# Cross-attention and mixture of experts on one core: unit 0's query in two halves, a reordered start, two loads on ScalarE's queue, 23 more filler transposes

## The chip, the cores and the metric

One core of a Trainium2 chip. The metric is the device time of one execution in microseconds (us), lower is better. Five engines run programs of their own (TensorE, VectorE, ScalarE, GpSimd, SyncE) and meet at semaphores. The profile gives the clock that was granted to TensorE in every stretch as a share of its full 2.4 GHz; 0.50 is 1.2 GHz.

## What is computed

x is 4 batches of 1024 rows of 256 floats; each batch has a context of 77 rows of 256. All is in fp32.

```python
def attention(q, k, v, mask):                    # 16 heads of 16
    qh, kh, vh = heads(q @ w_q + b_q), heads(k @ w_k + b_k), heads(v @ w_v + b_v)
    scores = where(mask == 0, -10000.0, qh @ kh.T * 16 ** -0.5)
    return merge(softmax(scores) @ vh) @ w_o + b_o
x = x + tanh(g_x) * attention(layernorm(x), ctx, ctx, mask)
xf = layernorm(x)
comb = top 2 of 4 of softmax(xf @ gate_w.T), rescaled to a sum of 1
y = sum over e: comb[:, e] * ((silu(xf @ eg[e].T) * (xf @ eu[e].T)) @ ed[e].T)
y = y + (silu(xf @ sg.T) * (xf @ su.T)) @ sd.T   # 688 wide inside, as each expert
x = x + tanh(g_f) * y
```

## The kernel before

**Work and its order.** The 4096 rows are 16 units of 256 rows, two tiles of 128. A unit goes through the attention, its second layernorm and the shared expert; the routed experts follow in a part of their own ("big tiles"), which the change does not touch. Each engine's program is one list written out by hand: a start, then `first_steps()` for units 0 to 3, then steps for the later units. An engine takes its instructions strictly in the order of its list, and each waits on counts of semaphores. A DMA belongs to the queue of the engine that issues it (SPq is SyncE's, ACTq ScalarE's) and occupies that engine while it is issued.

**One unit n.** The step names are those of the code, with the engine of each:
- `load_x` (L997), `load_mask` (L1002), SyncE: 256 KB of x, 77 KB of mask. `stats_1` (VectorE, L2037 to L2042) makes mean and variance, `rstd1` (GpSimd, L1150 to L1155) the scale, then x is normalised into xh: by ScalarE for unit 0 (L1538), by GpSimd for the later units (L1282, L1285).
- `x_T` (TensorE, L2736): four transposes into the PSUM bank p_m; `xT_copy` (ScalarE, L1545) copies them out; `q_T` (TensorE, L2744): eight matmuls by W_q, again into p_m.
- The query is kept as two parts of fewer bits each: `q_hi` (ScalarE, L1551) rounds p_m plus b_q, `q_lo` (VectorE, L2090) is the rest. p_m is free for its next user when q_lo has run; `prob_v(n)` waits for `q_lo(n + 2)`, for it uses p_m too.
- `scores(n, j)` (TensorE, L2763), j from 0 to 3: quarter j is tile j % 2 against the eight heads of half m = j // 2, which need only half m of the query and of the keys. It takes six matmuls (hi by hi, hi by lo, lo by hi, for two groups of four heads) into banks of p_s. `half_max(n, j)` (VectorE, L2108 and L2112) puts the masked entries to -10000 and takes the maxima; `exps(n, j)` (ScalarE, L1564) makes eight exps with their sums; `recip` (VectorE) and `normalise` (GpSimd, L1174) divide.
- `prob_T` (TensorE, L2782) and `t_copy` (ScalarE) transpose the probabilities; `prob_v(n)` (TensorE, L2797): 32 small matmuls against vblk. `out_proj`, `attended` and the second layernorm follow.

**The start.** SyncE loads, in this order, x of unit 0 (L997), the context (308 KB, L1054), W_k (256 KB, L1055), mask 0 (77 KB), W_q (256 KB, L1057), W_v (256 KB, L1058), x of unit 1, the gate's weights, mask 1, the shared expert's gate and up matrices (L1065, L1067), W_o, x of units 2 to 5, mask 2. ScalarE issues b_k and b_q (1 KB each, L1638, L1639), b_v (spread over 77 partitions, 77 KB, L1640), the two gates tgx and tgf (0.5 KB each) and b_o (128 KB, L1643). b_k, b_q and b_v count on one semaphore, s_bias, and both the keys (`keys_T`, L2185) and the query wait for all three (48 counts).

Keys: TensorE transposes the context (L2967 for batch 0, L2972 for the others; VectorE copies it out at L2196, L2199) and `keys_of` multiplies by W_k (L2979), batch 0 first. `keys_T` adds b_k and scales; ScalarE rounds (L1647, later L1655 for batches 1 to 3), VectorE takes the rest (L2191). The keys of a batch are then spread into blocks, one per half of the heads: `key_hi(m)` (VectorE, L2172) and `key_block` (GpSimd, L1178). Values: `values_of_context(half)` (TensorE), `context_values(k)` (VectorE, L2213, into vall); when both are done (s_vall 2), `place_values` (SyncE, L1013) copies batch 0's into vblk with 24 small DMAs within SBUF. `rest_of_start` (VectorE) is keys_T for batches 1 to 3, gwT, and two products with the gates.

`keep_warm(n)` (TensorE, L2962) is n transposes of the identity into p_t, whose result nobody reads; the kernel has 20 while x is loaded, two before keys_of and four before q_T(0). `w_T`, `w_hi` and `w_lo` transpose the shared expert's weights and split them in two parts; 11 groups of them lie between the steps of the first units.

The lists before, for unit 0 (each continues with unit 1):

```python
# VectorE: keys_T(0, 1); no_sight(0); keys_lo; key_hi(0); key_hi(1); q_lo(0); stats_1(1); then
half_max(0, 0) rest_of_start() context_values(0) context_values(1) half_max(0, 1) no_sight(1) stats_1(2)
half_max(0, 2) recip(0, 0) q_lo(1) recip(0, 1) w_lo(0) half_max(0, 3) w_lo(1) recip(0, 2) w_lo(2)
# ScalarE: normed(0); xT_copy(0); first keys rounded; q_hi(0); two tanh; then
exps(0, 0) xT_copy(1) other_keys_hi() exps(0, 1) q_hi(1) w_hi(0) exps(0, 2) w_hi(1) w_hi(2) exps(0, 3)
# TensorE: context transposes; keys_of(0, 1); x_T(0); q_T(0); keys_of(1, 4); gate's transposes; then
scores(0, 0) values_of_context(0), (1) scores(0, 1) x_T(1) scores(0, 2) q_T(1) w_T(0) scores(0, 3) w_T(1) w_T(2)
```

## Time and profile before

| | before |
|---|---|
| runs, us | 869.85, 868.10, 867.94; median 868.10 |
| profiled execution, us | 869.38 |
| its span, us | 867.7 |
| mean granted clock of TensorE | 0.991 |
| TensorE matmuls busy | 837.4 us, 97% |
| TensorE weight loads | 733.5 us, 85% |
| VectorE | 585.3 us, 67% |
| ScalarE | 522.0 us, 60% |
| GpSimd | 468.8 us, 54% |

The metric is the execution's time; the span goes from the first to the last instruction of the profile, and 1.7 us lie around it. Times in the trace count from the span's start. The shares are means over the whole span: they tell which engine is full most of the time and not what holds up a given step. A matmul's end is modelled, so a busy TensorE need not be at its peak.

### The profile page before, as it was taken

How to read it: one execution, taken by the hardware profiler on the slowest of the kernel's cores; microseconds unless marked ns; L12 is line 12 of the kernel's file. 1: busy time of each engine (PE TensorE's matmuls, PEld its weight loads, DVE VectorE, ACT ScalarE, POOL GpSimd, SP SyncE). 2: the span in 40 equal slices, each digit the busy share in tenths (PEclk: the TensorE clock that was granted, in tenths of full speed). 3: DMA queues.
4: the chain of work that ended last, by engine and by line, in shares of the span. 5: the costliest groups of instructions: out<-in, count | busy, mean ns of one | idle time of the engine just before them, and what ended most of it. 6: DMA issues, size and time to landing. Idle time of an engine off the chain costs nothing.

```text
span 867.7 us, 19215 instructions
## 1 busy us (share of the span) xinstructions
PE 837.4 (97%) x6183; PEld 733.5 (85%) x6184; DVE 585.3 (67%) x1214; ACT 522.0 (60%) x1846; POOL 468.8 (54%) x562
## 2 busy tenths in 40 slices
PE   8788899999999999999999999999999999999994
PEld 6567788888888799999988888888888888889994
DVE  6889889898888657976565666655665655454442
ACT  3989999999999635646565544445445454323231
POOL 5678678697575443666631444444444424364442
PEclk9899999999999999999999999999999999999998
DMA  7124323232222232323351444443444432232221
GB/s 222 41 79 122 117 68 98 85 106 83 76 90 63 75 109 71 119 91 113 102 153 39 76 75 71 69 65 64 69 68 68 73 50 38 31 49 42 36 42 19
DMA packets 104761, 67.84 MB, mean 78 GB/s; under 512 B 63514, under 2 KB 93055, under 8 KB 104671
## 3 DMA queue, kind: packets, MB, share of 16 engines
q1 hardware_dynamic: 90743, 48.93, 20.0%
q0 software_dynamic: 12864, 17.57, 12.6%
q8 instruction: 48, 0.79, 0.4%
q14 instruction: 42, 0.34, 0.1%
q10 hardware_dynamic: 1064, 0.21, 0.1%
HBM read 34.78 MB, written 25.82 MB: 70 GB/s over the span
## 4 chain that ended last, share of the span: by engine, by line
PE 86%; ACT 5%; DVE 3%; issue 2%; DMA 2%; POOL 0%; SPq 0%; DVEq 0%; ACTq 0%; POOLq 0%
PE p_s L680 23%; PE p_f L697 12%; PE p_f L2852 9%; PE p_s L347 7%; PE p_f L2897 4%; PE p_s L2852 4%; PE p_t L2782 3%; PE p_s L2763 3%; ACT prob L1564 3%; PE p_t L358 3%; PE p_m L2797 3%; PE p_m L2744 3%; PE p_m L2809 3%; PE p_s L2897 2%; PE p_s L2955 1%
## 5 line engine op out<-in xcount | busy, mean ns | idle before, releaser
L1564 ACT ACTIVATE prob<-p_s,negmax 128x77 f32<-128x77 f32 x512 | 161.7, 376 | 7.8 <-DVE negmax L2112 7.7
L1564 ACT ACTIVATION_READ_ACCUMULATOR prob<-p_s,negmax 128x1 f32 x512 | 129.9, 258 | 0.0
L537 POOL DMA_INDIRECT big_xin<-xn_scratch,slot_id x52 | 52.2, 1004 | 125.2 <-DMA big_placed<-big_xin 87.8
L581 ACT ACTIVATE big_sil<-p_s 128x512 f32<-128x512 f32 (+1 forms) x78 | 46.5, 596 | 115.7 <-PE p_s L680 102.2
L680 PE MATMUL p_s<-big_fxT_hi,big_w_hi 128*128 128x512 f32 (+1 forms) x286 | 112.8, 395 | 0.1
L680 PE MATMUL p_s<-big_fxT_lo,big_w_hi 128*128 128x512 f32 (+1 forms) x286 | 112.9, 395 | 0.0
L680 PE MATMUL p_s<-big_fxT_hi,big_w_lo 128*128 128x512 f32 (+1 forms) x286 | 112.2, 392 | 0.0
L1174 POOL TENSOR_TENSOR prob<-prob,rinv 128x616 f32<-128x616 f32 x64 | 78.9, 1237 | 58.6 <-DVE rinv L2119 58.6
L545 POOL DMA_INDIRECT out_rows<-big_yout,slot_id x52 | 85.9, 1652 | 43.8 <-DVE big_yout L643 28.2
L626 DVE TENSOR_TENSOR big_hid<-p_s,big_sil 128x512 f32<-128x512 f32 (+1 forms) x78 | 54.0, 692 | 76.8 <-ACT big_sil L581 72.0
L697 PE MATMUL p_f<-wd_hi,big_hT_hi 128*128 (+1 forms) x312 | 85.5, 280 | 0.0
L697 PE MATMUL p_f<-wd_lo,big_hT_hi 128*128 (+1 forms) x312 | 85.3, 279 | 0.0
L1193 POOL TENSOR_TENSOR shT_lo<-shid,shT_hi 128x256 fp32r<-128x256 f32 x80 | 63.2, 803 | 38.1 <-ACT shT_hi L1606 37.8
L2852 PE MATMUL p_f<-xnT_hi,swgu_hi 128*128 128x256 f32 x240 | 73.0, 304 | 0.0
L697 PE MATMUL p_f<-wd_hi,big_hT_lo 128*128 x260 | 72.7, 280 | 0.0
L633 DVE TENSOR_TENSOR big_hT_lo<-big_hid,big_hT_hi 128x512 fp32r<-128x512 f32 (+1 forms) x65 | 44.9, 691 | 35.6 <-ACT big_hT_hi L586 32.1
L2852 PE MATMUL p_f<-xnT_hi,swgu_lo 128*128 128x256 f32 x240 | 67.4, 281 | 0.0
L2852 PE MATMUL p_f<-xnT_lo,swgu_hi 128*128 128x256 f32 x240 | 67.3, 280 | 0.0
L680 PEld LDWEIGHTS p_s<-big_fxT_hi,big_w_lo 128*128 128x128 f32 (+1 forms) x286 | 53.0, 185 | 13.0
L586 ACT ACTIVATE big_hT_hi<-big_hid 128x512 fp32r<-128x512 f32 (+1 forms) x78 | 49.3, 632 | 23.2 <-DVE big_hid L626 18.8
L680 PEld LDWEIGHTS p_s<-big_fxT_hi,big_w_hi 128*128 128x128 f32 (+1 forms) x286 | 53.1, 186 | 10.3 <-issue 0.3
L2108 DVE COPY_PREDICATED_SCALAR p_s<-blind,hidden 128x616 f32 x64 | 54.8, 856 | 10.2 <-PE p_s L2763 9.7
(348 smaller groups left out, 2539.7 us busy)
## 6 DMA issues: line engine op xcount, KB each, us to landing
big_placed<-big_xin SPq DMA_DIRECT2D x176, 32.0 KB
xr<-in_x SPq DMA_DIRECT2D x16, 256.0 KB, 2.8
x_scratch<-xr SPq DMA_DIRECT2D x16, 256.0 KB, 2.4
xn_scratch<-xn SPq DMA_DIRECT2D x16, 256.0 KB, 2.1
xt_scratch<-xnT SPq DMA_DIRECT2D x16, 256.0 KB, 3.2
xin<-xt_scratch SPq DMA_DIRECT2D x16, 256.0 KB, 3.4
x1in<-x_scratch SPq DMA_DIRECT2D x16, 256.0 KB, 3.3
out_rows<-syout SPq DMA_DIRECT2D x16, 256.0 KB, 2.2
```

The lines of the kernel that those rows point to most:

```text
L347: last = nc.tensor.matmul(p_gu[:, g0:g1], fxT[a][:, c, :], wgu[b][:, bass.ds(e * KC + c, 1), g0:g1], start=(c == 0 and q == 0), stop=(c == ...
L537: pool.indirect_dma_start(xin[:, t, :], None, v["xn_d"], bass.IndirectOffsetOnAxis(slot_id[:, column(j, t)], 0)).then_inc(s_rows, 16)
L545: pool.indirect_dma_start(out, bass.IndirectOffsetOnAxis(slot_id[:, column(j, t)], 0), yout[:, t, :], None, compute_op=ALU.add).then_inc(s ...
L626: nc.vector.tensor_tensor(hid[n % 2][0:r, :], up, sil[n % 2][0:r, :], ALU.mult).then_inc(s_hid, 1)
L680: last = nc.tensor.matmul(p_gu[c % 2][half][0:out_rows, :], lhsT, fxT[j % 2][x][:, :, k, :], start=(k == 0 and q == 0), stop=(k == KC - 1 ...
L697: last = nc.tensor.matmul(p_y[t // 2][:, t % 2 * H:(t % 2 + 1) * H], hT[n % 3][h][0:r, at], wd[w][0:r, bass.ds(e * FC + c, 1), :], start=( ...
L1174: pool.tensor_tensor(pr_, pr_, rinv[:, t, m * HH:(m + 1) * HH].unsqueeze(2).broadcast_to([P, HH, SK]), ALU.mult).then_inc(s_P, 1)
L1193: pool.tensor_tensor(hT[1][:, c, :], hid[:, c, :], hT[0][:, c, :], ALU.subtract).then_inc(s_hlo, 1)
L1564: last = act.activation(prob[n % 2][t][:, m * PW + h * SK:m * PW + (h + 1) * SK], p_s[:, 2 * t + h // 4, col:col + SK], ACT.Exp, bias=negm ...
L2108: nc.vector.copy_predicated(sc, blind[:, n % 2, t, :].unsqueeze(1).unsqueeze(1).broadcast_to(shape), hidden[:, :].unsqueeze(2).unsqueeze(3 ...
L2852: last = nc.tensor.matmul(bank[:, j * UT * P:(j + 1) * UT * P], swgu[w][:, k, j * SGU + c * P:j * SGU + (c + 1) * P], xns[x][:, n % 2, k, ...
L2897: nc.tensor.matmul(bank[:, t * H:(t + 1) * H], hT[x][:, c, at], swd[w][:, c, :], start=(c == 0 and q == 0), stop=False)
```

## The change

**Loads.** The context and W_q are issued from ScalarE, ahead of b_k, b_q and b_v. SyncE's list is x, W_k, mask, W_v, x of unit 1 and so on.

**The query of unit 0** is made by halves. q_T(0) puts half 0 into p_m as before and half 1 into the bank p_f[1], and signals after each; q_hi(0) and q_lo(0) do and signal each half. For the later units nothing is split; only the counts grow by one (`queries(n)` is n + 2). scores(0, 0) and scores(0, 1) need half 0 alone, and key block 0 alone; scores(0, 2) needs both.

**The order of the lists.** VectorE makes key_hi(0) and half 0 of q_lo(0), then takes half_max(0, 0) and half_max(0, 1), and only then key_hi(1), the other half of q_lo, rest_of_start, half_max(0, 2), both context_values, recip(0, 0), no_sight(1), stats_1(2) and half_max(0, 3). ScalarE has exps(0, 1) ahead of xT_copy(1), and each later quarter one place earlier. TensorE has scores(0, 0) and scores(0, 1) right after q_T(0), ahead of keys_of(1, 4) and the gate's transposes; values_of_context(1), whose bank is p_f[1], waits for both halves of q_lo.

**Filler transposes.** 4 before scores(0, 3), 4 between w_T(0) and w_T(1), 9 between w_T(1) and w_T(2), 6 before scores(1, 0): 23. They use p_t, so TensorE waits before the first of them for the keys of all batches and for gwT, which are read from there.

```diff
         def four_banks(n, c):
             return n >= LATE or (n == LATE - 1 and c >= 2)
 
+        def queries(n):
+
+            return n + 2
+
+        def q_bank(n, m):
+            return p_f[1][:, 0:UT * P] if n == 0 and m == 1 else p_m[:, m * UT * P:(m + 1) * UT * P]
+
         def f_bank(n, c):
             use = 7 * n + c + (c >= 2)
             return wide_f[use % 4] if four_banks(n, c) else p_f[use % 2]
...
                 load_matrix(sp, v, raw[q % 2], s_raw[q % 2], q)
 
             load_x(0)
-            sp.dma_start(ctx_sb[:, :, :], v["ctx_in"].rearrange("b k d -> k b d")).then_inc(s_ctx, 16)
             sp.dma_start(wk[:, :, :], v["w_k"].rearrange("(c p) d -> p c d", p=P)).then_inc(s_wk, 16)
             load_mask(0)
-            sp.dma_start(wq[:, :, :], v["w_q"].rearrange("(c p) d -> p c d", p=P)).then_inc(s_wq, 16)
             sp.dma_start(wv[:, :, :], v["w_v"].rearrange("(c p) d -> p c d", p=P)).then_inc(s_wv, 16)
             load_x(1)
             sp.dma_start(gw_sb[:, :], v["gate_w"]).then_inc(s_gw, 16)
...
 
             def xT_copy(n):
                 act.wait_ge(s_xT, n + 1)
-                wait(act, s_q, n)
+                wait(act, s_q, queries(n - 1) if n > 0 else 0)
                 act.activation(xT[:, :, :], cols(p_m[:, :]), ACT.Copy).then_inc(s_xTc, 1)
 
             def q_hi(n):
-                act.wait_ge(s_q, n + 1)
                 wait(act, s_S, 4 * (n - 1))
                 for m in range(KC):
-                    last = act.activation(qT[0][:, n % 2, m, :], p_m[:, m * UT * P:(m + 1) * UT * P], ACT.Identity,
-                                          bias=bq[:, m:m + 1])
+                    if n == 0 or m == 0:
+                        act.wait_ge(s_q, m + 1 if n == 0 else queries(n))
+                    last = act.activation(qT[0][:, n % 2, m, :], q_bank(n, m), ACT.Identity, bias=bq[:, m:m + 1])
+                    if n == 0 and m == 0:
+                        last.then_inc(s_qhi, 1)
                 last.then_inc(s_qhi, 1)
 
             def exps(n, j, h0=0, h1=HH):
...
                 dst, src = e_part(G, 0)
                 act.activation(dst, src, ACT.Copy).then_inc(s_ehi, 1)
 
+            act.dma_start(ctx_sb[:, :, :], v["ctx_in"].rearrange("b k d -> k b d")).then_inc(s_ctx, 16)
+            act.dma_start(wq[:, :, :], v["w_q"].rearrange("(c p) d -> p c d", p=P)).then_inc(s_wq, 16)
             act.dma_start(bk[:, :], v["b_k"].rearrange("(c p) -> p c", p=P), allow_slow_non_contiguous=True).then_inc(s_bias, 16)
             act.dma_start(bq[:, :], v["b_q"].rearrange("(c p) -> p c", p=P), allow_slow_non_contiguous=True).then_inc(s_bias, 16)
             act.dma_start(bv[:, :], v["b_v"].partition_broadcast(SK)).then_inc(s_bias, 16)
...
 
             def first_steps():
                 exps(0, 0)
+                exps(0, 1)
                 xT_copy(1)
                 other_keys_hi()
-                exps(0, 1)
+                exps(0, 2)
                 q_hi(1)
                 w_hi(0)
-                exps(0, 2)
+                exps(0, 3)
                 w_hi(1)
                 w_hi(2)
-                exps(0, 3)
 
                 t_copy(0, 0)
                 w_hi(3)
...
+            def q_half_lo(n, m):
+                return nc.vector.scalar_tensor_tensor(
+                    out=qT[1][:, n % 2, m, :], in0=q_bank(n, m), scalar=bq[:, m:m + 1], in1=qT[0][:, n % 2, m, :],
+                    op0=ALU.add, op1=ALU.subtract)
+
             def q_lo(n):
-                dve.wait_ge(s_qhi, n + 1)
-                for m in range(KC):
-                    last = nc.vector.scalar_tensor_tensor(
-                        out=qT[1][:, n % 2, m, :], in0=p_m[:, m * UT * P:(m + 1) * UT * P], scalar=bq[:, m:m + 1],
-                        in1=qT[0][:, n % 2, m, :], op0=ALU.add, op1=ALU.subtract)
-                last.then_inc(s_qlo, 1)
+                dve.wait_ge(s_qhi, queries(n))
+                q_half_lo(n, 0)
+                q_half_lo(n, 1).then_inc(s_qlo, 1)
 
             def no_sight(n):
                 dve.wait_ge(s_mask[n % 2], 16 * (n // 2 + 1))
...
             no_sight(0)
             keys_lo(0, 1, 0)
             dve.wait_ge(s_own, 3)
-            for m in range(KC):
-                key_hi(m)
-            q_lo(0)
+            key_hi(0)
+            dve.wait_ge(s_qhi, 1)
+            q_half_lo(0, 0).then_inc(s_qlo, 1)
             stats_1(1)
 
             def context_values(k):
...
 
             def first_steps():
                 half_max(0, 0)
+                half_max(0, 1)
+                key_hi(1)
+                dve.wait_ge(s_qhi, queries(0))
+                q_half_lo(0, 1).then_inc(s_qlo, 1)
                 rest_of_start()
+                half_max(0, 2)
                 context_values(0)
                 context_values(1)
-                half_max(0, 1)
+                recip(0, 0)
                 no_sight(1)
                 stats_1(2)
-                half_max(0, 2)
-                recip(0, 0)
+                half_max(0, 3)
                 q_lo(1)
                 recip(0, 1)
                 w_lo(0)
-                half_max(0, 3)
                 w_lo(1)
                 recip(0, 2)
                 w_lo(2)
...
             def x_T(n):
                 pe.wait_ge(s_xh, n + 1)
                 wait(pe, s_x1, n - 2)
-                wait(pe, s_qlo, n)
+                wait(pe, s_qlo, queries(n - 1) if n > 0 else 0)
                 for k in range(KC):
                     for t in range(UT):
                         last = nc.tensor.transpose(p_m[:, (k * UT + t) * P:(k * UT + t + 1) * P],
...
                 pe.wait_ge(s_xTc, n + 1)
                 for m in range(KC):
                     for k in range(KC):
-                        last = nc.tensor.matmul(p_m[:, m * UT * P:(m + 1) * UT * P], wq[:, k, m * P:(m + 1) * P],
+                        last = nc.tensor.matmul(q_bank(n, m), wq[:, k, m * P:(m + 1) * P],
                                                 xT[:, k, :], start=(k == 0), stop=(k == KC - 1))
+                    if n == 0 and m == 0:
+                        last.then_inc(s_q, 1)
                 last.then_inc(s_q, 1)
 
             def scores(n, j):
                 t, m = j % 2, j // 2
                 b = n // UB
                 wait(pe, s_exp, 4 * n + j - 1)
-                if j == 0:
-                    pe.wait_ge(s_qlo, n + 1)
+                if n == 0 and j == 0:
+                    pe.wait_ge(s_qlo, 1)
+                elif j == 0 or (n == 0 and j == 2):
+                    pe.wait_ge(s_qlo, queries(n))
                 if b == 0:
                     pe.wait_ge(s_kbhi, m + 1)
                     pe.wait_ge(s_kblo, m + 1)
...
-                pe.wait_ge(s_qlo, min(n + 3, NU))
+                pe.wait_ge(s_qlo, queries(min(n + 2, NU - 1)))
...
             x_T(0)
             keep_warm(4)
             pe.wait_ge(s_wq, 16)
+            pe.wait_ge(s_ctxT, 1 + KC)
             q_T(0)
-            pe.wait_ge(s_ctxT, 1 + KC)
+            scores(0, 0)
+            scores(0, 1)
             keys_of(1, B, p_t)
             pe.wait_ge(s_gw, 16)
             for k in range(KC):
...
                 last.then_inc(s_vps, 1)
 
             def first_steps():
-                scores(0, 0)
                 values_of_context(0)
-                values_of_context(1)
-                scores(0, 1)
                 x_T(1)
                 scores(0, 2)
+                pe.wait_ge(s_qlo, queries(0))
+                values_of_context(1)
                 q_T(1)
+                pe.wait_ge(s_kT, 4)
+                pe.wait_ge(s_gwT, 2)
+                keep_warm(4)
+                scores(0, 3)
                 w_T(0)
-                scores(0, 3)
+                keep_warm(4)
                 w_T(1)
+                keep_warm(9)
                 w_T(2)
+                keep_warm(6)
 
                 scores(1, 0)
                 w_T(3)
```

## Rows read from the trace of the kernel before

**Rows 1.** Stretches of 20 us: engines' busy us (instructions), PEclk, DMA share, GB/s.

```profile
60.00:80.00 20.00, 17.78 (x184) 12.96 (x173) 18.55 (x37) 19.14 (x102) 15.31 (x21) 1.00 0.34 107
...
100.00:120.00 20.00, 19.98 (x184) 17.03 (x183) 17.86 (x41) 18.86 (x93) 16.50 (x25) 1.00 0.29 85
```

**Rows 2.** Timeline of the DMA issues: start, duration in us, queue, line.

```profile
0.81 0.50 ACTq L1638 DMA_DIRECT2D bk<-in_L_xattn_b_k  x1
...
1.32 0.45 SPq L1054 DMA_DIRECT2D ctx_sb<-in_ctx  x1
...
2.76 0.47 SPq L1057 DMA_DIRECT2D wq<-in_L_xattn_w_q  x1
...
3.27 0.59 SPq L1058 DMA_DIRECT2D wv<-in_L_xattn_w_v  x1
...
3.45 0.64 ACTq L1643 DMA_DIRECT2D bog<-in_L_xattn_b_o  x1
```

**Rows 3.** Timeline, 9 to 14 us: start, us, engine, line; in brackets idle before.

```profile
8.96 0.50 DVE L2185 TENSOR_SCALAR kT<-p_s,bk 128x77 f32<-128x77 f32 x2 [0.95 <-PE p_s L2979]
9.12 0.47 PEld L2962 LDWEIGHTS p_t<-ident 128*128 128x128 f32 x4
...
9.43 0.60 ACT L1545 ACTIVATE xT<-p_m 128x512 f32<-128x512 f32 x1 [0.75 <-PE p_m L2736]
9.92 0.33 ACT L1647 ACTIVATE kT_hi<-kT 128x154 fp32r<-128x154 f32 x1
...
10.52 2.53 DVE L2172 TENSOR_TENSOR kblk_hi<-kT_hi,own 128x616 fp32r<-128x616 f32 x2
10.75 3.38 POOL L1178 TENSOR_TENSOR kblk_lo<-kT_lo,own 128x616 fp32r<-128x616 f32 x2 [3.19 <-DVE kT_lo L2191]
...
10.98 1.99 PE L2744 MATMUL p_m<-xT,wq 128*128 128x256 f32 x8 [1.16 <-DMA wq<-in_L_xattn_w_q]
...
13.08 0.84 ACT L1551 ACTIVATE qT_hi<-p_m,bq 128x256 fp32r<-128x256 f32 x2 [2.83 <-PE p_m L2744]
```

**Rows 4.** Timeline, 15 to 22 us: first maximum, first and second exps, the context's values.

```profile
15.86 0.86 DVE L2108 COPY_PREDICATED_SCALAR p_s<-blind,hidden 128x616 f32 x1
...
17.59 0.33 ACT L1564 ACTIVATE prob<-p_s,negmax 128x77 f32<-128x77 f32 x1 [3.49 <-DVE negmax L2112]
...
18.72 1.29 DVE L2213 TENSOR_TENSOR vall<-p_f,bv 77x512 f32<-77x512 f32 x2
...
21.73 0.33 ACT L1564 ACTIVATE prob<-p_s,negmax 128x77 f32<-128x77 f32 x1 [0.23 <-DVE negmax L2112]
```

**Rows 5.** Timeline of SyncE's queue, 18 to 62 us.

```profile
20.04 18.75 SPq L1013 DMA_DIRECT2D vblk<-vall  x24
```

**Rows 6.** Timeline of TensorE: prob_v(0), prob_v(1).

```profile
42.12 3.61 PE L2797 MATMUL p_m<-pT,vblk 128*32 128x256 f32 x32 [0.46 <-DVE qT_lo L2090]
...
59.96 1.93 PE L2797 MATMUL p_m<-pT,vblk 128*32 128x256 f32 x32
```

**Rows 7.** Short stretches, columns as in rows 1.

```profile
24.00:28.00 4.00, 1.80 (x12) 1.13 (x12) 3.57 (x8) 4.00 (x23) 3.77 (x6) 1.00 0.07 7
...
34.00:35.00 1.00, 1.00 (x5) 0.82 (x4) 0.44 (x2) 1.00 (x7) 0.82 (x1) 0.50 0.05 5
38.00:42.00 4.00, 2.25 (x16) 1.52 (x16) 3.62 (x7) 4.00 (x26) 2.06 (x2) 1.00 0.45 103
...
43.00:45.00 2.00, 2.00 (x25) 1.22 (x20) 1.14 (x5) 2.00 (x14) 1.24 (x2) 0.50 0.11 17
```

**Rows 8.** DMA issues in 0 to 22 us: median us from issue to landing.

```profile
wv<-in_L_xattn_w_v SPq DMA_DIRECT2D x1, 256.0 KB, 8.6
```

**Rows 9.** Chain of waits: start, us, what; one quarter of scores.

```profile
77.50 0.69 PE p_s L2763 x6
```

**Rows 10.** Timeline of GpSimd, 24 to 38 us.

```profile
25.57 1.04 POOL L1285 TENSOR_TENSOR xh<-xh,nb 128x512 f32<-128x512 f32 x1
```

**Rows 11.** Line 1013 alone, 18 to 62 us: duration ns min/median/max.

```profile
L1013 SPq DMA_DIRECT2D vblk<-vall x30: 545/756/954, 20.0 to 43.9; - x30
```

More of the change, by code:

```diff
@@ L2816, in xn_T @@
                 pe.wait_ge(s_x1, n + 1)
-                pe.wait_ge(s_qlo, min(n + 4, NU))
+                pe.wait_ge(s_qlo, queries(min(n + 3, NU - 1)))
                 for k in range(KC):
```

## The prediction

> **What bounds it now.** The page's first part has TensorE busy for nearly all of the span, so the next question is where it is not. Stretches of 20 us answer: 17.8 of 20 us from 60 to 80, and 19.98 from 100 to 120 [rows 1]; of the 34 such stretches from 120 to 800 only one is under 19.3. From about 100 us on TensorE has no gap, so the change can only move the time at which that full stretch begins, one for one; the steps behind it are unaltered. Before 100 us ScalarE is the fullest (19.1 of 20 us, [rows 1]), fed by VectorE's maxima. The start is what the diff rewrites, so I read it as a timeline, and set the changed order's durations end to end against it.
>
> The start has four marks. W_q's load is issued at 2.76 and TensorE waits for it until 10.98 [rows 2, 3]. The first exps begin at 17.59, the context's values are done at 20.0, and at 20.04 SyncE starts 24 DMA issues that put them into vblk; they take 18.75 us [rows 4, 5]. prob_v(0), the first reader of vblk, runs at 42.12 after q_lo(2), for 3.61 [rows 6]. The clock is at its lower level (1.2 GHz, granted 0.50) at 34 to 35 and again at 43 to 45, and at the upper one in the 4 us before each of the two falls, in which TensorE was busy for 1.80 and 2.25 us [rows 7].
>
> **Loads.** Before, SyncE issues x, context, W_k, mask, W_q; context (0.45) and W_q (0.47) go to the head of ScalarE's queue, ahead of b_k, b_q, b_v, which so leave 1.0 later [rows 2]. ScalarE has time: its issues ended at 4.1 [rows 2], and the copy of x's transposes had waited 0.75 when it ran at 9.43 [rows 3]. SyncE's later loads leave 0.5 to 1.0 earlier. W_q passes the mask and no longer decides: the end of that copy does, at 10.03, plus some 0.2 for sharing with the context. What gets late is b_v. keys_T(0, 1) needs the three biases; it ran at 8.96, so they had landed by then [rows 3]. Now 564 KB stand before them in their own queue. Until W_q landed at 10.94, 1153 KB of SyncE's loads (x 256, context 308, W_k 256, mask 77, W_q 256, by the tensors' sizes) and 208 KB of ScalarE's had gone with it: 134 KB per us from the first issues at 0.81. If the two queues take turns, 643 KB of each must pass before b_v is in: 1286 KB, or 10.4 us. Bounds: 9.0 (no delay) and 11.9 (when W_v, behind as much, landed: 3.27 plus 8.6, [rows 2, 8]). I take 10.5. The Trainium skill, page "DMA: Bandwidth & Descriptors", section "Issuing engines are not separate DMA queues", says that DMAs of all engines share the same 16 engines, and that a second issuer saves issue time alone; by it the context and W_q are paid for by what stands behind them, and the sum would have b_v at the late bound, 1.4 us more. The rows do show the two queues in flight together, and no more.
>
> **Unit 0.** Keys 0.50, their rounded copy 0.33, the rest as much, one key block on GpSimd 1.7 at most [rows 3]: 10.5 + 2.9 = 13.4. Half of the query is there by 12.3, since q_T is 2.0 whole and q_hi 0.43 a half. scores(0, 0) 13.4 to 14.1 (0.69, [rows 9]); maximum 1.7 (15.86 to the exp's start, [rows 4]); exps(0, 0) at 16.0 where it was 17.59: 1.6 earlier. The second maximum ends at 17.7 and its exps(0, 1), now at 21.73 [rows 4], follow exps(0, 0) without the gap, at 18.2: 3.5 earlier. So far the change does what it says.
>
> **What is queued behind it on VectorE.** After the second maximum (17.7) come key_hi(1) 1.0 (2.53 for two beside GpSimd's, [rows 3]), half of q_lo 0.45, rest_of_start 1.1 (17.6 to 18.72), half_max(0, 2) 1.7 and its wait 0.2, and only then both context_values 1.3 [rows 4]: they end at 23.4, which was 20.0. stats_1(2) stands behind them and ends at 24.8; GpSimd's xh(2), made from it, is then ready at 28.8 instead of 26.6, and normalise(0, 0) starts that much later [rows 10]. The lead is gone by unit 1.
>
> **SyncE.** Its 24 issues move with the values: 23.4 + 18.75 = 42.2, and the last piece lands about 1.1 later (between 0 and the 3.3 between the last issue's end and prob_v(0), which did not wait for it). prob_v(0) so starts at 43.3 and not at 42.12: 1.2 later. Here one wait takes the place of another, and all slack of the way to it is swallowed, the cold clock's too.
>
> **Fillers.** 23 transposes at 0.117 (0.47 for four, [rows 3]) are 2.7 us of TensorE. Four stand before scores(0, 3), whose reader VectorE is free at 24.9 while the scores are done at 24.85; 13 stand between w_T(0) and w_T(2), which wait for ScalarE's exps and VectorE's rounding; six before scores(1, 0), 2 us ahead of its maximum. I cost them at nothing; if that cover were gone, at 0.47, 1.5 and 0.7. They fill the stretch before the first fall of the clock [rows 7] and should keep it at 2.4 GHz up to 35. What that gives on TensorE ends in the wait for vblk. Nothing is put into 36 to 43, where TensorE has the same 2.25 of 4 us as now, or less with the wait at its end. So I expect the second fall again, with prob_v(0) at 3.6 us and not the 1.93 of prob_v(1) at the upper level [rows 6].
>
> **Sum.** prob_v(0) starts 1.2 later; being later, its end reaches back into the upper level, minus 0.3; the rest follows one for one: 0.9 later. The profiled execution took 869.4 (span 867.7 and 1.7 around it), so a like execution gives 870.3. The median of the three runs is 868.1, 1.3 below that; nothing ties the 1.3 to the start, so I carry it: 869.0. As a run without the first fall loses nothing of what varies there, I put 869.2. Two thousandths (1.7 us, 866.4 and 869.8) is about what a measurement of this kernel can tell from no change.
>
> **Rivals.** (a) *The clock holds through prob_v(0).* For it: fillers before, and only 1.2 us more of gap. Against: the 2.25 of 4 us. 43.3 + 1.93 = 45.2 against 45.7: 0.5 earlier, 867.7. (b) *Slower: the biases.* If b_v lands at 12.0, ScalarE's copy, both key blocks, all maxima and the values go 1.5 later, prob_v(0) starts at 44.8, and the longer gap keeps the lower level over scores(2, 0) and out_proj(0) too (some 1.9 us of matmuls at the upper): 2.7 later at its start, 2.0 to 3.5 at its end: 871.0. It decides once the biases are later than 10.5. (The skill's section "Queues, rings and completion order" on the same page has each DMA engine take turns between queues packet by packet; the tiny packets of b_k and b_q would then each cost a turn against 1 KB of SyncE's.) (c) *Faster: vblk is not late.* The issues took 545 to 954 ns each [rows 11]. At 545, 24 of them end at 36.5 and prob_v(0) waits for q_lo(2) only, at 41.9; with the clock up it ends at 43.8, 1.9 earlier: 866.2. It decides below 0.72 us an issue, and needs the clock as well. (d) *The change does not do what it says*: the biases are so late that exps(0, 0) stays at 17.6; that is the end of (b).
>
> **Chances.** The forecast 0.42 (0.08 of it above 869.8), (a) 0.15, (b) 0.28, (c) 0.15. Faster is (c) 0.15; slower is (b) and the top of the forecast, 0.36; the rest, 0.49, is the same. The range goes from 866.9 (part of (c) left out) to 871.6 (the early half of (b)'s late end in). The forecast's own is 868.2 to 870.4.
>
> **What would show it.** keys_T(0, 1) waiting for a DMA until about 10.5, scores(0, 0) near 13.4, exps(0, 0) near 16.0; values done at 23.4 and SyncE's vblk issues from there to 42.2; prob_v(0) near 43.3 with its waiting put down to a DMA; the clock whole at 28 to 35 and at 0.50 again at 43 to 45; TensorE full from about 101. It is wrong if keys_T is not delayed, if prob_v(0) starts before 42.5, or if prob_v(0) takes 1.9.

## The result, and the profile after

| | before | after |
|---|---|---|
| runs on the same chips, median us | 868.62 (13 runs) | 871.32 (13 runs) |
| profiled execution, us | 869.38 | 871.42 |
| its span, us | 867.7 | 869.7 |
| TensorE matmuls busy, us | 837.4 | 839.7 |
| VectorE busy, us | 585.3 | 585.2 |

The ratio is 1.0030, with a 95% interval of 1.0022 to 1.0038: the change makes the kernel 2.7 us slower. No engine's busy time grew by more than the fillers. The time is lost before 48 us and carried to the end: scores(2, 0) starts 1.66 later (47.31 against 45.65) and scores(5, 2) 1.69 later (106.57 against 104.88), one for one as the prediction had it. The two profiled executions differ by 2.0 and not by 2.7: before's lay 0.8 above its median, after's 0.1.

The start, from the timeline of the changed kernel (columns as in [rows 3]):

```profile
9.71 0.50 DVE L2196 TENSOR_SCALAR kT<-p_s,bk 128x77 f32<-128x77 f32 x2 [2.19 <-DMA bv<-in_L_xattn_b_v]
...
10.55 0.60 ACT L1550 ACTIVATE xT<-p_m 128x512 f32<-128x512 f32 x1 [1.21 <-PE p_m L2750]
...
11.29 1.64 PE L2758 MATMUL p_m<-xT,wq 128*128 128x256 f32 x4
...
13.54 0.48 DVE L2097 SCALAR_TENSOR_TENSOR qT_lo<-p_m,bq,qT_hi 128x256 fp32r<-128x256 f32 x1 [1.11 <-ACT qT_hi L1557]
...
16.79 0.33 ACT L1571 ACTIVATE prob<-p_s,negmax 128x77 f32<-128x77 f32 x1 [2.30 <-DVE negmax L2123]
```

Against [rows 3] and [rows 4]: the keys waited 2.19 us for b_v and ran at 9.71 instead of 8.96, the copy of x's transposes at 10.55 instead of 9.43. The first exp still comes 0.80 earlier, at 16.79, since only half of the query is needed; the second quarter's exps followed at 19.21 instead of 21.73.

What came of that lead stands on VectorE and GpSimd, 21 to 35 us of the timeline:

```profile
21.40 0.86 DVE L2119 COPY_PREDICATED_SCALAR p_s<-blind,hidden 128x616 f32 x1 [0.43 <-PE p_s L2781]
...
23.01 1.27 DVE L2224 TENSOR_TENSOR vall<-p_f,bv 77x512 f32<-77x512 f32 x2
...
26.52 0.86 DVE L2119 COPY_PREDICATED_SCALAR p_s<-blind,hidden 128x616 f32 x1 [0.95 <-PE p_s L2781]
...
28.24 1.04 POOL L1290 TENSOR_TENSOR xh<-xh,nb 128x512 f32<-128x512 f32 x1
...
29.24 3.57 POOL L1179 TENSOR_TENSOR prob<-prob,rinv 128x616 f32<-128x616 f32 x3
...
31.05 0.34 DVE L2174 TENSOR_TENSOR swgu_lo<-p_f,swgu_hi 128x176 fp32r<-128x176 f32 x1 [1.39 <-ACT swgu_hi L1624]
...
32.15 1.15 DVE L2202 TENSOR_TENSOR kT_lo<-kT,kT_hi 128x462 fp32r<-128x462 f32 x1
33.22 0.85 DVE L2119 COPY_PREDICATED_SCALAR p_s<-blind,hidden 128x616 f32 x1
```

The last row is half_max(1, 0): 33.22, where it was 30.55. VectorE is to be seen waiting three times (0.43, 0.95, 1.39) where it had been nearly full. The same stretch of both kernels, from the start of half_max(0, 0) to the start of half_max(1, 0), says it in two rows (columns as in rows 1). Before:

```profile
15.86:30.55 14.69, 11.90 (x70) 8.38 (x69) 13.93 (x30) 12.46 (x70) 13.53 (x22) 0.93 0.25 75
```

After:

```profile
15.06:33.22 18.16, 15.87 (x103) 12.03 (x103) 15.06 (x32) 13.64 (x73) 13.52 (x22) 1.00 0.24 73
```

The stretch is 3.47 us longer. VectorE is busy 1.13 more in it (15.06 against 13.93: key_hi(1), 1.17, and half of q_lo, 0.47, now lie inside instead of ahead; other steps take less, keys_lo by 0.18) and idle 2.34 more (3.10 against 0.76).

Two ways lead to half_max(1, 0). One goes over GpSimd: stats_1(2) stands behind half_max(0, 2) and both context_values in VectorE's new list, xh(2) is made from it, and normalise(0, 0) can start only then, 12.45 behind the first exp instead of 8.98. That is the same 3.47. The other goes over ScalarE, which now has w_hi(1) and w_hi(2) behind exps(0, 3) (first its timeline in the changed kernel, then that of the kernel before):

```profile
28.25 0.33 ACT L1571 ACTIVATE prob<-p_s,negmax 128x77 f32<-128x77 f32 x1 [1.12 <-DVE negmax L2123]
...
30.67 0.84 ACT L1624 ACTIVATE swgu_hi<-p_f 128x176 fp32r<-128x176 f32 x2
```

```profile
27.74 0.92 ACT L1617 ACTIVATE swgu_hi<-p_f 128x176 fp32r<-128x176 f32 x2
```

w_hi(1), the first of the two in that row, starts 13.88 behind the first exp instead of 10.15, and w_lo(1) on VectorE waits 1.39 for it.

The rest of the way, from the timeline of TensorE, VectorE and SyncE:

```profile
24.32 18.75 SPq L1020 DMA_DIRECT2D vblk<-vall  x24
...
38.14 0.63 PE L2800 MATMUL p_t<-ident,prob 128*128 128x128 f32 x4 [1.65 <-ACT pT L1580]
...
39.84 1.09 PE L2800 MATMUL p_t<-ident,prob 128*128 128x128 f32 x4 [0.46 <-ACT pT L1580]
...
41.71 1.09 PE L2800 MATMUL p_t<-ident,prob 128*128 128x128 f32 x4 [0.78 <-ACT pT L1580]
...
43.44 0.87 DVE L2097 SCALAR_TENSOR_TENSOR qT_lo<-p_m,bq,qT_hi 128x256 fp32r<-128x256 f32 x2
...
44.45 2.93 PE L2815 MATMUL p_m<-pT,vblk 128*32 128x256 f32 x32 [0.27 <-DVE qT_lo L2097]
```

And short stretches (columns as in rows 1):

```profile
9.00:12.00 3.00, 2.60 (x10) 2.22 (x11) 1.25 (x5) 1.16 (x3) 0.13 (x1) 0.50 0.73 234
...
28.00:32.00 4.00, 2.64 (x22) 1.91 (x20) 2.57 (x8) 3.26 (x18) 3.92 (x5) 1.00 0.05 4
...
36.00:38.00 2.00, 0.48 (x3) 0.08 (x1) 1.41 (x4) 2.00 (x12) 1.48 (x2) 1.00 0.06 5
38.00:42.00 4.00, 2.63 (x16) 1.90 (x17) 2.96 (x7) 3.96 (x17) 2.92 (x6) 0.71 0.04 4
42.00:46.00 4.00, 3.73 (x28) 2.38 (x30) 3.05 (x5) 3.51 (x24) 0.72 (x1) 0.50 0.39 84
```

The fillers kept the clock up at 28 to 35, where it had fallen. In this execution it was also at the lower level at 9 to 12, where it had been up before. It now falls at 39.7 and stays at the lower level to 46.5 (28.6 to 35.4 and 42.2 to 45.6 before): the two groups of transposes behind the fall take 1.09 instead of 0.63. prob_v(0) runs at 44.45 and waits for q_lo(2); vblk's last piece had landed at 44.18, only 0.27 ahead.

**The sum by marks.** Single executions differ by 1 to 2 us in how early the loads land and where the low clock lies at the start, so I measure from the first exp, exps(0, 0). Starts behind it, in us:

| | exps(0, 0) at | exps(0, 3) | half_max(1, 0) | exps(1, 0) | prob_v(0) | scores(2, 0) |
|---|---|---|---|---|---|---|
| before | 17.59 | 10.82 | 12.96 | 14.68 | 24.52 | 28.06 |
| after | 16.79 | 11.45 | 16.43 | 18.15 | 27.66 | 30.52 |

So 0.80 is won up to the first exp, 3.47 is lost from there to exps(1, 0), and 1.01 is won between exps(1, 0) and scores(2, 0) (12.37 against 13.38): 1.66 in all. Of the 1.01, 0.68 is prob_v(0) itself, 2.93 us instead of 3.61, since the clock is back at its upper level from 46.5 on, before it ends; 0.33 lies ahead of it.

### The profile page after: what moved, and what is told of

Same layout as the page of the kernel before. It is cut to its first block, busy times and chain, and to the rows that moved or that the text cites. A ratio compares the mean times of both kernels' runs of the same rounds, so it can differ in the third digit from the quotient of the medians.

```text
span 869.7 us, 19263 instructions
## 1 busy us (share of the span) xinstructions
PE 839.7 (97%) x6206; PEld 735.2 (85%) x6207; DVE 585.2 (67%) x1214; ACT 522.3 (60%) x1846; POOL 467.1 (54%) x562
## 3 DMA queue, kind: packets, MB, share of 16 engines
q0 software_dynamic: 12864, 17.57, 12.5%
## 4 chain that ended last, share of the span: by engine, by line
PE 86%; ACT 4%; DVE 4%; issue 2%; DMA 1%; POOL 1%; DVEq 0%; SPq 0%; ACTq 0%; POOLq 0%
PE p_s L680 23%; PE p_f L697 12%; PE p_f L2870 9%; PE p_s L347 7%; PE p_f L2915 4%; PE p_s L2870 4%; PE p_t L2800 3%; PE p_s L2781 3%; PE p_t L358 3%; PE p_m L2827 3%; PE p_m L2815 3%; ACT prob L1571 3%; PE p_m L2758 2%; PE p_s L2915 2%; PE p_s L2973 1%
## 5 line engine op out<-in xcount | busy, mean ns | idle before, releaser
L1571 ACT ACTIVATION_READ_ACCUMULATOR prob<-p_s,negmax 128x1 f32 x512 | 132.3, 264 | 0.0
L581 ACT ACTIVATE big_sil<-p_s 128x512 f32<-128x512 f32 (+1 forms) x78 | 46.5, 596 | 114.9 <-PE p_s L680 114.9
L545 POOL DMA_INDIRECT out_rows<-big_yout,slot_id x52 | 85.2, 1638 | 43.3 <-DVE big_yout L643 29.6
L697 PE MATMUL p_f<-wd_hi,big_hT_lo 128*128 x260 | 72.7, 280 | 0.0
```

The costliest lines, as they stand in the source:

```text
L545: pool.indirect_dma_start(out, bass.IndirectOffsetOnAxis(slot_id[:, column(j, t)], 0), yout[:, t, :], None, compute_op=ALU.add).then_inc(s ...
L697: last = nc.tensor.matmul(p_y[t // 2][:, t % 2 * H:(t % 2 + 1) * H], hT[n % 3][h][0:r, at], wd[w][0:r, bass.ds(e * FC + c, 1), :], start=( ...
L1571: last = act.activation(prob[n % 2][t][:, m * PW + h * SK:m * PW + (h + 1) * SK], p_s[:, 2 * t + h // 4, col:col + SK], ACT.Exp, bias=negm ...
```

## The experiments

The theories to tell apart: prob_v(0) is late because of vblk (the forecast's), because of the clock, because of the loads, or because of the chain over VectorE and GpSimd that ends in exps(1, 0) and q_lo(2). Ratios are to the kernel before, run beside each group of experiments: 868.51 us for e1 to e4, 868.23 for e5 to e8, 868.29 for e9 to e12. Each kernel has one profile, so the marks rest on one execution each.

**e1: no fillers.** The changed kernel, its four keep_warm calls in first_steps left out.

```diff
-                keep_warm(4)
                 scores(0, 3)
                 w_T(0)
-                keep_warm(4)
                 w_T(1)
-                keep_warm(9)
                 w_T(2)
-                keep_warm(6)
```

> The changed kernel without its 23 filler transposes. Theory (a chain on VectorE and ScalarE sets prob_v(0)): four fillers stand between q_T(1) and scores(0, 3), whose maximum VectorE waited 0.95 us for, so exps(0, 3) and all behind it move up by up to 0.5; without fillers the clock is at its lower level somewhere in 28 to 35 again, as in the kernel before. Both effects are small and of opposite sign: 870.8 to 871.6 us. Rival (the clock decides): the fillers saved the fall at 28 to 35 but the fall at 39.7 to 46.5 took its place; without them the fall sits at 28 to 35, prob_v(0) takes about 2 us at the upper level: 870.0 or less.

Measured 870.82 us, 1.0026 (1.0016 to 1.0036) of the kernel before. exps(0, 3) comes 11.03 behind the first exp instead of 11.45, so four fillers did cost 0.42. half_max(1, 0) and exps(1, 0) did not move: 16.42 and 18.14. Something else than the chain over exps(0, 3) held them. The rows, from this kernel's timeline of GpSimd and VectorE:

```profile
28.07 3.56 POOL L1179 TENSOR_TENSOR prob<-prob,rinv 128x616 f32<-128x616 f32 x3
...
30.55 1.57 DVE L2202 TENSOR_TENSOR kT_lo<-kT,kT_hi 128x462 fp32r<-128x462 f32 x1
```

keys_lo started 0.43 earlier against the first exp and took 1.57 instead of 1.15. It ended at 32.12, 0.49 behind GpSimd's third normalise (31.63). After: 33.30 and 32.81, again 0.49.

The clock was at its lower level at 28.5 to 35.3 and 42.1 to 45.5, as in the kernel before, and scores(2, 0) still came 12.38 behind exps(1, 0), against 12.37 with the fillers: the 1.01 won there doesn't come from the first fall's absence.

**e2: loads back**, and **e3: loads only.** The change's two lines, undone in the changed kernel and made alone in the kernel before.

```diff
             load_x(0)
+            sp.dma_start(ctx_sb[:, :, :], v["ctx_in"].rearrange("b k d -> k b d")).then_inc(s_ctx, 16)
             sp.dma_start(wk[:, :, :], v["w_k"].rearrange("(c p) d -> p c d", p=P)).then_inc(s_wk, 16)
             load_mask(0)
+            sp.dma_start(wq[:, :, :], v["w_q"].rearrange("(c p) d -> p c d", p=P)).then_inc(s_wq, 16)
...
-            act.dma_start(ctx_sb[:, :, :], v["ctx_in"].rearrange("b k d -> k b d")).then_inc(s_ctx, 16)
-            act.dma_start(wq[:, :, :], v["w_q"].rearrange("(c p) d -> p c d", p=P)).then_inc(s_wq, 16)
```

> The changed kernel with context and W_q loaded from SyncE again. Theory: the moved loads made x (first statistics 5.55 instead of 4.89), the biases (keys_T at 9.71 instead of 8.96) and the copy of x's transposes (10.55 instead of 9.43) late and lowered the clock at 9.0 to 12.4; with them back q_T(0) runs at 10.98 at the upper level, scores(0, 0) at 13.1, exps(0, 0) at 15.8, and the whole chain to prob_v(0), the values and their 24 issues among it, comes 1.0 earlier: 870.4 us. Rival (the lead is lost behind unit 0 anyway, at half_max(1, 0), by waits that don't go back to the start): exps(0, 0) earlier by 1.0 but prob_v(0) by under 0.3: 871.2.

> The kernel before with only the two loads moved to ScalarE. Theory: keys and the transposes of x 1.1 later, key blocks done at 14.5, q_lo(0) at 15.1, scores(0, 0) at 15.3 instead of 14.88, and 0.4 to 1.1 later for everything up to prob_v(0): 869.1 to 869.7 us. Rival (the loads are harmless, W_q's earlier landing makes up for it): 868.6.

e2 took 871.20 us (1.0028, 1.0017 to 1.0040), e3 869.28 (1.0008, 0.9997 to 1.0019). Neither differs clearly from the kernel it was made of. e2's profile shows why a single one can't decide: its clock was at the lower level up to 14.05, so its first exp came at 17.52, later than after's. From exps(0, 0) to exps(1, 0) it took 18.16, e3 14.68: the loads have no part in the 3.47.

**e4: fillers only.** The kernel before with the 23 fillers (and their wait for p_t) among w_T(0), w_T(1), w_T(2) and scores(1, 0).

```diff
                 q_T(1)
+                pe.wait_ge(s_kT, 4)
+                pe.wait_ge(s_gwT, 2)
+                keep_warm(4)
                 w_T(0)
                 scores(0, 3)
+                keep_warm(4)
                 w_T(1)
+                keep_warm(9)
                 w_T(2)
+                keep_warm(6)
```

> The kernel before with only the 23 fillers, at the same places among the weights' transposes. If the clock is what the fillers buy: no lower level in 28 to 35, the transposes and scores(1, 1) there at full speed, and prob_v(0) no earlier than q_lo(2), which waits for ScalarE's exps, so 0 to 0.6 earlier there. Theory: as in the changed kernel the fall moves behind them, to 38 to 46, and gives it back: 868.3 to 869.0 us. Rival: the clock stays up through prob_v(0) as well, which then ends 1.9 earlier: 866.7.

867.85 us, 0.9990 (0.9980 to 1.0000): somewhat better than expected, at the edge of what can be told. The clock stayed up from 11.0 to 41.75 and fell there; prob_v(0) took 3.60 once more. scores(2, 0) came 27.14 behind the first exp, 0.92 less than before.

**e5: vblk early.** The changed kernel; SyncE's issues for batch 0 wait for the first half of the values, and VectorE makes that half earlier.

```diff
-                sp.wait_ge(s_vall, 2)
+                sp.wait_ge(s_vall, 2 if b > 0 else 1)
...
                 q_half_lo(0, 1).then_inc(s_qlo, 1)
+                context_values(0)
                 rest_of_start()
                 half_max(0, 2)
-                context_values(0)
                 context_values(1)
```

> The changed kernel with vblk's 24 issues set free by the first half of the values alone, whose sum VectorE makes right behind the query's second half. The issues run from about 20.7 to 39.5 and the last piece lands near 40.6 instead of 44.18. My theory now: prob_v(0) waits for q_lo(2), which is late because GpSimd's third normalise ends 16.0 after the first exp (12.5 before) and holds VectorE's keys_lo and half_max(1, 0) behind it; so nothing is gained: exps(1, 0) 18.1 to 18.4 behind exps(0, 0), 871.0 to 871.6 us. Rival (the forecast's own: vblk is the wait that sets prob_v(0)): prob_v(0) 1.2 earlier, 870.1.

**e6: keys_lo late.** The changed kernel with one line moved on VectorE.

```diff
-                keys_lo(1, B, 1)
 
                 half_max(1, 0)
+                keys_lo(1, B, 1)
```

> The changed kernel with keys_lo of batches 1 to 3 behind half_max(1, 0) on VectorE instead of ahead of it. Theory: keys_lo took 1.15 because it waited for GpSimd's normalise to end (it ended 0.48 or 0.49 behind it in three kernels); behind half_max(1, 0), with GpSimd idle, it takes under 0.8, and half_max(1, 0) starts 15.4 behind exps(0, 0) instead of 16.43: exps(1, 0) 1.0 earlier. prob_v(0) then waits for vblk, 0.25 earlier: 871.0 us. Rival (ScalarE's exps(0, 3) and w_hi set the pace): half_max(1, 0) no earlier than 16.2.

**e7: both.**

```diff
-                sp.wait_ge(s_vall, 2)
+                sp.wait_ge(s_vall, 2 if b > 0 else 1)
...
+                context_values(0)
                 rest_of_start()
...
                 half_max(1, 0)
+                keys_lo(1, B, 1)
```

> Both edits together. Theory of two waits side by side at prob_v(0) (q_lo(2) at 44.3, vblk at 44.2): only both together give the time back, prob_v(0) 0.9 to 1.0 earlier against exps(0, 0) than in the changed kernel: 870.4 us. Rival (the clock's fall at 39.7 eats it, since TensorE's gaps stay): under 0.3, 871.1.

e5: 870.78 us (1.0030, 1.0021 to 1.0039). vblk had landed at 40.23, 4 us ahead, and prob_v(0) started where it did, 27.68 behind the first exp:

```profile
44.36 2.97 PE L2815 MATMUL p_m<-pT,vblk 128*32 128x256 f32 x32 [0.27 <-DVE qT_lo L2097]
```

e6: 871.36 us (1.0041, 1.0027 to 1.0056). half_max(1, 0) moved to 15.39 and exps(1, 0) to 17.14, 1.01 earlier, and prob_v(0) only to 27.50. Now it waits for the DMA, from VectorE's and TensorE's timeline of e6:

```profile
29.95 0.34 DVE L2174 TENSOR_TENSOR swgu_lo<-p_f,swgu_hi 128x176 fp32r<-128x176 f32 x1 [1.39 <-ACT swgu_hi L1624]
...
31.05 0.85 DVE L2119 COPY_PREDICATED_SCALAR p_s<-blind,hidden 128x616 f32 x1
...
32.65 0.63 DVE L2202 TENSOR_TENSOR kT_lo<-kT,kT_hi 128x462 fp32r<-128x462 f32 x1
...
43.15 3.39 PE L2815 MATMUL p_m<-pT,vblk 128*32 128x256 f32 x32 [1.25 <-DMA vblk<-vall]
```

So GpSimd's way gave back 1.0 of the 3.47. half_max(1, 0) (31.05) now starts right behind w_lo(2), and w_lo(1) still waits 1.39 for w_hi(1). The other 2.4 stands with the way over ScalarE. No run put w_hi(1) and w_hi(2) back ahead of exps(0, 3), so that part is read from the rows and not shown. In the changed kernel w_T(1) had ended at 27.23, and ScalarE stood idle for the 1.12 before exps(0, 3).

e7: 870.01 us (1.0022, 1.0013 to 1.0031). prob_v(0) at 26.57 and scores(2, 0) at 29.45, 1.07 earlier than after. Each wait alone gives nothing (0.02 the wrong way and 0.16), both together 1.09: they stand side by side, and the forecast named only one. The 1.09 rests on the marks of one profile each. The whole times agree with it but don't prove it, since e7's interval still overlaps the change's (1.0022 to 1.0038). keys_lo itself takes 0.63 with GpSimd idle: 0.52 of its 1.15 was waiting for normalise, which no row puts down as a wait. The Trainium skill has a rule for it on the page "SBUF — State Buffer", section "Who interferes with whom": a tensor_tensor of VectorE with both inputs in SBUF contends with GpSimd's reads of SBUF, the port pair that the two share is an exclusive lock, and the order of issue decides which of them blocks. The traces agree: in all eleven profiles in which keys_lo runs beside normalise it takes 1.14 to 1.57 and ends 0.49 or 0.50 behind it, and in the other three it takes 0.63.

**e8: late fillers.** The kernel before with e4's 23 fillers and 14 more ahead of prob_T(0, 3), prob_T(0, 4) and prob_v(0), where TensorE waited; they write into banks whose last reader is waited for.

```diff
+            def warm_f(k, done, count):
+                pe.wait_ge(s_wlo, done)
+                for n in range(count):
+                    nc.tensor.transpose(p_f[k][:, n % 4 * P:(n % 4 + 1) * P], ident[:, :], ident[:, :])
...
                 scores(1, 2)
+                warm_f(1, 4, 3)
                 prob_T(0, 3)
+                warm_f(1, 4, 8)
                 prob_T(0, 4)
                 w_T(5)
                 scores(1, 3)
+                warm_f(0, 5, 3)
                 prob_v(0)
```

> The kernel before with the 23 fillers and 14 more in the gaps ahead of prob_T(0, 3), prob_T(0, 4) and prob_v(0), in banks that nobody holds there. Theory: TensorE is busy through 36 to 42, the clock does not fall there, prob_v(0) takes 1.93 instead of 3.6, and scores(2, 0) comes 1.5 to 2.0 earlier: 866.0 to 866.9 us. Rival (the fillers delay what stands behind them as much as the clock gives): 867.9, as with the 23 alone.

865.73 us, 0.9969 (0.9959 to 0.9978): 2.5 us faster than the kernel before and, by the two ratios, some 5.3 faster than the change. Its windows and prob_v(0):

```profile
38.00:42.00 4.00, 3.57 (x40) 2.40 (x42) 3.62 (x7) 4.00 (x27) 1.79 (x2) 1.00 0.54 127
42.00:46.00 4.00, 3.47 (x38) 2.37 (x31) 3.46 (x10) 4.00 (x26) 3.39 (x4) 1.00 0.34 97
```

```profile
40.89 1.93 PE L2797 MATMUL p_m<-pT,vblk 128*32 128x256 f32 x32
```

TensorE is busy for 3.57 of the 4 us in which it had been busy for 2.25 [rows 7], the clock is at its upper level without a break from 5.5 to 858.8 us, and prob_v(0) takes 1.93. scores(2, 0) is at 25.46, 2.60 earlier than before and 1.68 earlier than e4.

**e9 and e10: late fillers on the changed kernel**, alone and with e7's two edits. As in e8, with 12 more ahead of prob_T(0, 2), since TensorE waits 1.65 there.

```diff
                 q_T(2)
+                warm_f(1, 4, 12)
                 prob_T(0, 2)
                 scores(1, 2)
+                warm_f(1, 4, 3)
                 prob_T(0, 3)
+                warm_f(1, 4, 8)
                 prob_T(0, 4)
                 w_T(5)
                 scores(1, 3)
+                warm_f(0, 5, 3)
                 prob_v(0)
```

> The changed kernel with 26 more fillers in TensorE's gaps ahead of prob_T(0, 2), prob_T(0, 3), prob_T(0, 4) and prob_v(0). The clock should not fall at 39.7 any more. prob_v(0) is then held by vblk, whose last piece lands 27.4 behind exps(0, 0), and takes 1.93: scores(2, 0) 29.4 behind exps(0, 0) instead of 30.5, 870.2 us. Rival (the fillers delay the transposes they stand before, or q_lo(2) sets prob_v(0) alone and comes 1 us earlier with the clock): 871.3 on the one side, 869.2 on the other.

> The changed kernel with vblk early, keys_lo behind half_max(1, 0) and the same 26 fillers. Theory: prob_v(0) about 26.5 behind exps(0, 0), scores(2, 0) at 28.4 to 28.6 (29.45 without the fillers): 868.9 us, the same as the kernel before within 0.2%, and still 3 behind the kernel before with 37 fillers, since exps(1, 0) stays 17.7 behind exps(0, 0) against 14.7. Rival (the lists' new order is as good as the old one once the waits and the clock are mended): 866.5 or less.

e9: 868.56 us (1.0000, 0.9991 to 1.0009; one of its twelve executions took 4648 us, for a reason that nothing here shows, and is not in the ratio). prob_v(0) waits for vblk and takes 1.93, scores(2, 0) comes at 29.34, as expected:

```profile
44.59 1.93 PE L2815 MATMUL p_m<-pT,vblk 128*32 128x256 f32 x32 [0.41 <-DMA vblk<-vall]
```

The whole is 1.6 better than expected, and 0.9 of it lies far behind: from out_proj(15) to the first matmul of the routed experts this profile takes 146.6 us, after's 147.5. Of all fourteen profiles four take 146.6 to 146.8 (e8, e9, e10, e12), e5 147.0 and nine 147.3 to 148.0; the step lies at the logits' transposes near 320 us. I have no cause for it. e8's profile has it too: of the 3.6 us between its span and before's, 0.7 lies there. e10: 867.73 us (0.9992, 0.9982 to 1.0001), scores(2, 0) at 27.72. exps(1, 0) is at 16.73 and not at the 17.7 that I had taken from e7, where b_v had landed only at 11.50 (9.57 in e10) and the clock was at its lower level at 15.3 to 18.7, and exps(0, 2) came 7.73 behind the first exp instead of 6.31. With both waits and the clock mended, the new lists are still 2.3 behind the old ones (25.46).

**e11: the 14 late fillers alone**, on the kernel before (e8 without e4's edit), and **e12: e8 with the two loads on ScalarE**, the second diff against e8.

```diff
                 scores(1, 2)
+                warm_f(1, 4, 3)
                 prob_T(0, 3)
+                warm_f(1, 4, 8)
                 prob_T(0, 4)
                 w_T(5)
                 scores(1, 3)
+                warm_f(0, 5, 3)
```

```diff
-            sp.dma_start(ctx_sb[:, :, :], v["ctx_in"].rearrange("b k d -> k b d")).then_inc(s_ctx, 16)
...
-            sp.dma_start(wq[:, :, :], v["w_q"].rearrange("(c p) d -> p c d", p=P)).then_inc(s_wq, 16)
...
+            act.dma_start(ctx_sb[:, :, :], v["ctx_in"].rearrange("b k d -> k b d")).then_inc(s_ctx, 16)
+            act.dma_start(wq[:, :, :], v["w_q"].rearrange("(c p) d -> p c d", p=P)).then_inc(s_wq, 16)
```

> The kernel before with the 14 late fillers alone, without the 23. Theory: the clock falls once, in 27 to 35, where TensorE's lower speed hides behind ScalarE's and VectorE's full stretches, and stays up through prob_v(0): scores(2, 0) 26.4 to 26.9 behind exps(0, 0), 867.0 us; the 23 early ones are worth 0.5 to 1.2 beside them. Rival (the early ones are worth nothing): 865.8.

> The kernel before with all 37 fillers, and the context and W_q loaded from ScalarE. With the clock steady the loads' own effect should stand out. Theory: biases and x's transposes later, the query's matmuls no earlier than 10.6: 866.2 to 866.6 us, 0.5 to 0.9 above the same kernel with the loads on SyncE. Rival (harmless): 865.7.

e11: 867.41 us (0.9982, 0.9973 to 0.9991). scores(2, 0) at 25.47, the same as e8; the 23 early fillers are not what brings it there. In this profile the clock fell at 28.4 for half as long as before and once more at 72.7 to 76.2, after which it is 1.2 behind e8. Whether the early fillers prevent that later fall, one profile can't say; the medians differ by 1.7, the ratios by 1.1 us, with intervals that overlap. e12: 865.69 us (0.9974, 0.9965 to 0.9982), 0.04 from e8 by the medians and 0.4 by the ratios. That is nearer to the rival: no harm of the loads is to be seen in the old order, though the intervals leave room for the 0.5 that the theory wanted.

## Why the prediction was right or wrong

The measured 871.3 lies in the range (866.9 to 871.6) but above the forecast's own (868.2 to 870.4); "the same", given the most chance, was wrong, and slower, at 0.36, was right. It came out near rival (b)'s number, 2.7 later, and not by (b)'s way. That the range holds it is therefore in part luck.

- *Only the start counts, one for one.* Right: 1.66 at scores(2, 0), 1.69 at scores(5, 2).
- *b_v at 10.5, keys 13.4, first exp at 16.0.* The wait for b_v was there, but it ended at 9.7, nearer to the bound of no delay; in five other profiles with the change's lists and loads it landed at 9.5 to 9.6, and in e7 at 11.5, near the late bound. The first exp came at 16.79 in this profile and at 15.63 to 17.52 in the seven other profiles of the changed lists. Not in the sum: the lower clock at 9.0 to 12.4, at which x's transposes and most of q_T ran. Rival (b) did not happen in this profile. Its first link, the late b_v, did in e7, and the first exp came at 17.30 there.
- *exps(0, 1) without the gap.* Right, 2.42 behind the first.
- *The queue behind it on VectorE.* Right in size: values done 7.5 behind the first exp (forecast 7.4), xh(2) ready at 29.28 (28.8). The 28.8 doesn't follow from its own terms: from stats_1(2) to xh(2) it is 3.7 in both traces, which makes 28.5, or 12.5 behind the first exp, as measured.
- *The step that failed: "normalise(0, 0) starts that much later … The lead is gone by unit 1".* I named it and gave it no price, taking all slack up to prob_v(0) to be swallowed by vblk. Its price is 3.47 from exps(0, 0) to exps(1, 0). VectorE's queue was as long as forecast; what hangs on it behind normalise(0, 0) was left out of the sum. The third normalise ends 16.0 behind the first exp (12.5 before) and holds keys_lo (e1, e6), and w_lo(1) waits for exps(0, 3) in ScalarE's new order (read from the rows, not tested). This puts q_lo(2) at 44.3, behind the 43.3 at which I had prob_v(0).
- *SyncE's issues: values + 18.75, landing 1.1 later.* Right: 24.32 + 18.75 = 43.07, landed 44.18. But it was not the wait that set prob_v(0) (e5); it stood 0.27 behind it as the next one (e6), so that only e7 gave anything back.
- *Fillers at nothing.* Four cost 0.42 at exps(0, 3), within the price named for the cover gone; nothing of it reached exps(1, 0) (e1).
- *The clock.* The first fall went, as forecast. The second came earlier and lasted twice as long (39.7 to 46.5). Ahead of it TensorE was busy for 0.48 of the 2 us from 36 to 38, where it waited for t_copy(0, 1), behind exps(1, 0) on ScalarE; that this brought the fall forward is likely but not shown, for e1, with exps(1, 0) just as late and no fillers, fell at 28.5 and again at 42.1. Being later, prob_v(0) did reach back into the upper level: 0.7 won, where the sum had 0.3. Rival (a) needed fillers there: with them the clock holds (e9), as the 3.57 of 4 us in e8 shows too.

## What to carry to other kernels

Work moved behind the critical step on the same engine is paid for there: VectorE was full (13.93 of 14.69 us), so the 1.64 us that left the way to the first maximum came back in the way to the fifth, and waits that the new order opened were added to it (2.34). When two waits end within 0.3 us of each other, price both, and test both edits together; singly each looks worthless. Filler transposes paid off where a gap stood ahead of work that is long at the lower clock (e8: 1.7 us at prob_v(0)), and less in an earlier gap, behind which the clock fell all the same (e4).

## What the runs showed of the hardware

- VectorE's keys_lo, both inputs in SBUF, took 0.63 with GpSimd idle (e6, e7, e10) and 1.14 to 1.57 beside its normalise (the eleven other profiles), always ending 0.49 or 0.50 behind it. The trace shows this as duration and not as a wait.
- With 37 identity transposes in TensorE's gaps between 22 and 41 us, and no other change, the clock was at its upper level from 5.5 to 858.8 us (e8), and from 6.6 to 856.5 with the two loads moved as well (e12); without them it fell twice in between. It is one profile each.
- Where the clock is low at the start differs from one execution to the next: after, e1, e6 and e9 run the same instructions up to the first exp, and the clock fell at 9.0 to 12.4 in the first, at 9.9 to 13.3 in e9 and not at all there in e1 and e6. Their first exps came at 15.6 to 17.1.
